# Scaling gate and up products in place in PSUM, with the low-rank matmul accumulated onto them

## What is computed

```
def _qlinear(x, q, scale, A, Bm):
    w = (q.astype(jnp.float32) - Q_ZERO) * (scale * Q_STEP)[:, None]
    y = jnp.einsum('bsh,oh->bso', x, w)
    return y + LR_SCALE * (x @ A @ Bm)
g = _qlinear(x, gate_q, gate_scale, gate_A, gate_B)
u = _qlinear(x, up_q, up_scale, up_A, up_B)
h = jax.nn.silu(g) * u
return _qlinear(h, down_q, down_scale, down_A, down_B)
...
x = x + 0.5 * _L0_ffn_ref(_layernorm(x), ...)
x = x + _L0_attn_ref(_layernorm(x), ...)
x = x + 0.5 * _L0_ffn_ref(_layernorm(x), ...)
```

## Time and profile before

| | |
|---|---|
| median of 3 runs | 631.45 us (631.31 to 633.48) |
| span of the profiled execution | 632.9 us |
| busy PE, DVE, ACT, POOL | 601.7, 457.9, 270.9, 72.3 us |
| instructions on PE, DVE, ACT, POOL | 3070, 851, 505, 89 |
| mean granted TensorE clock | 0.992 of full speed |
| DMA | 35.46 MB |

### The profile page before, as it was taken

One profiled execution on the slowest core, in us unless ns is written; L12 is line 12 of the kernel. 1 busy time (PEld: TensorE's weight loads), 2 busy tenths in 40 slices (PEclk: granted clock), 3 DMA queues, 4 the chain that ended last, 5 costly groups with the idle time before them and its releaser, 6 DMA issues.

```text
span 632.9 us, 9273 instructions
## 1 busy us (share of the span) xinstructions
PE 601.7 (95%) x3070; PEld 290.9 (46%) x3070; DVE 457.9 (72%) x851; ACT 270.9 (43%) x505; POOL 72.3 (11%) x89
## 2 busy tenths in 40 slices
PE   3798899999999999999997999999999999999997
PEld 2443444444444545444454544444454444544443
DVE  6699949895788868793698589548874688556643
ACT  3765303662066404561563366216640565126620
POOL 4236800000000001000064000000000000000000
PEclk9999989999999999999997999999999999999999
DMA  8984120004000210000278000300031001250001
GB/s 298 395 279 132 39 46 1 2 1 76 8 0 0 50 33 2 1 1 2 49 140 141 21 2 1 75 9 2 1 55 29 0 0 27 56 200 0 1 9 59
DMA packets 67620, 35.46 MB, mean 56 GB/s; under 512 B 56160, under 2 KB 60448, under 8 KB 67584
## 3 DMA queue, kind: packets, MB, share of 16 engines
q1 hardware_dynamic: 66768, 34.87, 21.0%
q10 hardware_dynamic: 816, 0.14, 0.1%
HBM read 17.43 MB, written 4.19 MB: 34 GB/s over the span
## 4 chain that ended last, share of the span: by engine, by line
PE 79%; DVE 8%; issue 1%; ACT 1%; DVEq 1%; ACTq 0%
PE bank L1047 41%; PE bank L1025 22%; PE bank L1004 5%; PE bank L1065 5%; PE bank L981 2%; PE bank L1144 2%; PE bank L1126 1%; PE bank L1013 1%; DVE z L627 1%; DVE work L708 1%; DVE zs L620 1%; DVE X L670 1%; DVE X L911 1%; DVE uq_raw L667 0%; DVE z L629 0%
## 5 line engine op out<-in xcount | busy, mean ns | idle before, releaser
L512 ACT ACTIVATE work<-bank,scales 128x512 f32<-128x512 f32 (+1 forms) x176 | 120.3, 684 | 173.8 <-PE bank L1047 173.3
L1047 PE MATMUL bank<-xT,gw 128*128 128x512 f16 (+1 forms) x696 | 164.4, 379 | 0.8 <-ACT work L512 0.8
L1047 PE MATMUL bank<-xT,uw 128*128 128x512 f16 (+1 forms) x696 | 164.4, 379 | 0.0
L1025 PE MATMUL bank<-dw,hT 128*128 128x512 f16 (+1 forms) x704 | 160.6, 381 | 0.0
L1047 PEld LDWEIGHTS bank<-xT,gw 128*128 128x128 f16 (+1 forms) x696 | 69.4, 100 | 81.2 <-ACT work L512 1.6
L1047 PEld LDWEIGHTS bank<-xT,uw 128*128 128x128 f16 (+1 forms) x696 | 69.7, 100 | 79.8
L1025 PEld LDWEIGHTS bank<-dw,hT 128*128 128x128 f16 (+1 forms) x704 | 68.1, 98 | 78.6 <-issue 2.2
L690 DVE SCALAR_TENSOR_TENSOR work<-bank,work 128x512 f32<-128x512 f32 (+1 forms) x88 | 60.6, 688 | 27.2 <-ACT work L512 21.3
L703 DVE SCALAR_TENSOR_TENSOR work<-bank,work 128x512 f32<-128x512 f32 (+1 forms) x88 | 60.4, 686 | 20.8 <-ACT work L512 20.4
L708 DVE TENSOR_TENSOR work<-work 128x512 f32<-128x512 f32 (+1 forms) x88 | 63.7, 724 | 4.7 <-ACT work L535 1.3
L648 DVE SCALAR_TENSOR_TENSOR hT<-work,hT 128x512 f16<-128x512 f32 (+1 forms) x88 | 61.2, 695 | 6.1 <-ACT hT L517 5.6
(11 more groups left out here) (145 smaller groups left out, 436.7 us busy)
## 6 DMA issues: line engine op xcount, KB each, us to landing
out_x<-X SPq DMA_DIRECT2D x16, 256.0 KB, 2.1
X<-in_x SPq DMA_DIRECT2D x1, 2048.0 KB, 14.8
gq_raw<-in_tables SPq DMA_DIRECT2D x1, 2048.0 KB, 11.7
gq_raw<-in_gate_q_t SPq DMA_DIRECT2D x2, 768.0 KB, 11.3
uq_raw<-in_up_q_t SPq DMA_DIRECT2D x2, 768.0 KB, 11.3
dq_raw<-in_down_q_t SPq DMA_DIRECT2D x1, 1536.0 KB, 14.6
work<-in_b SPq DMA_DIRECT2D x2, 688.0 KB, 8.4
X<-in_x SPq DMA_DIRECT2D x4, 256.0 KB, 5.3
```

The source lines that it names most:

```text
L512: return nc.scalar.activation(out, in_, ACT.Copy, scale=scales[0:rows[m], g, m:m + 1])
L1025: last = mm(bank[4 + b][:, :], hT[0:rows[m], m, a, j * P:(j + 1) * P], dw[0:rows[m], m, :], start=(m == 0 and a == 0), stop=(m == M - 1 an ...
L1047: last = mm(dst[0:r, :], w[:, c, cols], xT[:, a, c, :], start=(c == 0 and a == 0), stop=(c == KH - 1 and a == 1))
```

## The change

The gate product of block m goes to bank 0 or 2 and up's to bank 1 or 3, by m % 2. ACT multiplies each by its channel factor in place, PSUM to PSUM. The low-rank matmul of a block is issued one block later, without clearing, so that it adds to the scaled bank. Silu reads the gate bank, DVE multiplies its result with the up bank. L690 and L703 and four SBUF tiles are gone. The common factor `LR_OUT` moves into silu's scale, `h_high`, `h_low` and the channel factors. `pd_product` uses bank 2. At the end of a tile `down_half(n, 0, 0)` stands between the two halves of `pd_product`.

```diff
@@ scalar
-            def scaled(out, in_, g, m):
-                return nc.scalar.activation(out, in_, ACT.Copy, scale=scales[0:rows[m], g, m:m + 1])
+            def scaled(acc, g, m):
+                return nc.scalar.activation(acc, acc, ACT.Copy, scale=scales[0:rows[m], g, m:m + 1])
...
+            def gate_silu(n, m):
+                b, r = m % 2, rows[m]
+                act.wait_ge(f.gl_mm, n * M + m + 1)
+                after(act, f.h[b], uses(n, m))
+                nc.scalar.activation(silu[0:r, b, :], gate_bank[b][0:r, :], ACT.Silu, scale=LR_OUT)\
+                    .then_inc(f.silu[b], 1)
...
                 for m in range(M):
-                    b, r, k = m % 2, rows[m], uses(n, m)
+                    b, r = m % 2, rows[m]
                     act.wait_ge(f.g_mm, n * M + m + 1)
-                    after(act, f.g[b], k)
-                    scaled(tg[0:r, b, :], bank[0][0:r, :], 0, m).then_inc(f.tg[b], 1)
+                    scaled(gate_bank[b][0:r, :], 0, m).then_inc(f.tg[b], 1)
+                    if m:
+                        gate_silu(n, m - 1)
+                    act.wait_ge(f.u_mm, n * M + m + 1)
+                    scaled(up_bank[b][0:r, :], 1, m).then_inc(f.tu[b], 1)
                     if m:
                         h_high(n, m - 1)
...
+                gate_silu(n, M - 1)
                 h_high(n, M - 1)
@@ vector
-                    dve.wait_ge(f.tg[b], k + 1)
-                    dve.wait_ge(f.gl_mm, n * M + m + 1)
-                    after(dve, f.silu[b], k)
-                    V.scalar_tensor_tensor(g32[0:r, b, :], bank[2][0:r, :], c, tg[0:r, b, :],
-                                           ALU.mult, ALU.add).then_inc(f.g[b], 1)
+                    dve.wait_ge(f.ul_mm, n * M + m + 1)
+                    dve.wait_ge(f.silu[b], k + 1)
+                    after(dve, f.hlo[b], k)
+                    V.tensor_tensor(h32[0:r, b, :], silu[0:r, b, :], up_bank[b][0:r, :], ALU.mult)\
+                        .then_inc(f.h[b], 1)
                     if m:
                         h_low(n, m - 1)
...
@@ tensor
             def pd_product(n, half):
 
                 if half == 0:
-                    pe.wait_ge(f.tg[(M - 1) % 2], uses(n, M - 1) + 1)
+                    pe.wait_ge(f.silu[M % 2], uses(n, M - 2) + 1)
                     pe.wait_ge(f.hlo[0], uses(n, M - 3) + 1)
                     pe.wait_ge(f.hlo[1], uses(n, M - 4) + 1)
...
+                def product(g, m):
+                    b, r, cols = m % 2, rows[m], slice(m * P, m * P + rows[m])
+                    w, dst, done = ((gw, gate_bank[b], f.g_mm), (uw, up_bank[b], f.u_mm))[g]
+                    after(pe, (f.silu, f.h)[g][b], uses(n, m))
...
+                def low_rank(g, m):
+                    b, r, cols = m % 2, rows[m], slice(m * P, m * P + rows[m])
+                    w, dst, done = ((gb_w, gate_bank[b], f.gl_mm), (ub_w, up_bank[b], f.ul_mm))[g]
+                    pe.wait_ge((f.tg, f.tu)[g][b], uses(n, m) + 1)
...
+                    mm(dst[0:r, :], w[:, cols], PT[:, g, :], start=False, stop=True,
+                       skip_group_check=True).then_inc(done, 1)
+
+                started = first and n == 0
                 for m in range(M):
...
+                    for g in range(2):
+                        if not (started and m == 0):
+                            product(g, m)
+                        if m:
+                            low_rank(g, m - 1)
                     if s4 and m == 2:
                         cauchy(n)
...
                 pd_product(n, 0)
+                for g in range(2):
+                    low_rank(g, M - 1)
+                down_half(n, 0, 0)
                 pd_product(n, 1)
                 if more:
                     p_product(n + 1, 0)
-                down_half(n, 0, 0)
                 if more:
                     p_product(n + 1, 1)
                 down_half(n, 0, 1)
@@ sync
             def transposes(n):
 
-                sp.wait_ge(f.ul_mm, n * M)
+                sp.wait_ge(f.u_mm, n * M)
```

More of the change, by code:

```diff
@@ L243, in s4_macaron @@
         c_out = [sem(f"conv_out_{j}") for j in range(TS)]
+        gate_bank, up_bank = (bank[0], bank[2]), (bank[1], bank[3])
         c_bank = [bank[4], bank[5], bank[2], bank[3]]
@@ L500, in pd_high @@
                 after(act, f.dl_mm, n * TS)
-                nc.scalar.activation(PdT[:, :], bank[0][:, :], ACT.Copy,
+                nc.scalar.activation(PdT[:, :], bank[2][:, :], ACT.Copy,
                                      scale=1.0 / (H_SCALE * A_SCALE)).then_inc(f.pd_hi, 1)
@@ L699, in tile @@
                         down_a()
[L700 to L709, removed]
                     if more and m in (1, 3, 6, 8):
@@ L1003, in pd_product @@
                     for a in range(2):
-                        last = mm(bank[0][:, :], da_w[0:rows[m], m, :, :].rearrange("p a r -> p (a r)"),
+                        last = mm(bank[2][:, :], da_w[0:rows[m], m, :, :].rearrange("p a r -> p (a r)"),
                                   hT[0:rows[m], m, a, :], start=(m == 0 and a == 0),
@@ L1031, in tile @@
             def tile(n, more, s4=False, first=False):
-                for m in range(M):
[L1035 to L1069, removed]
-                        product(0)
-                    if not late:
-                        low_rank(0)
-                    if not started:
-                        product(1)
-                    if late:
-                        low_rank(0)
-                    low_rank(1)
@@ new lines, in product @@
+                def product(g, m):
+                    b, r, cols = m % 2, rows[m], slice(m * P, m * P + rows[m])
+                    w, dst, done = ((gw, gate_bank[b], f.g_mm), (uw, up_bank[b], f.u_mm))[g]
+                    after(pe, (f.silu, f.h)[g][b], uses(n, m))
+                    if m == 0 and g == 1:
+                        pe.wait_ge(f.p_stack, n * TS + TS)
+                    if first and m == 1 and g == 0 and n != 0:
+                        for out_read in c_out:
+                            pe.wait_ge(out_read, SUBS // TS)
+                    if isinstance(n, int) and n == 0:
+                        pe.wait_ge((s_gcast, s_ucast)[g], 1 + sum(m >= m1 for _, m1 in CHUNKS))
+                    for c in range(KH):
+                        for a in range(2):
+                            last = mm(dst[0:r, :], w[:, c, cols], xT[:, a, c, :],
+                                      start=(c == 0 and a == 0), stop=(c == KH - 1 and a == 1))
+                    last.then_inc(done, 1)
@@ new lines, in low_rank @@
+                def low_rank(g, m):
+                    b, r, cols = m % 2, rows[m], slice(m * P, m * P + rows[m])
+                    w, dst, done = ((gb_w, gate_bank[b], f.gl_mm), (ub_w, up_bank[b], f.ul_mm))[g]
+                    pe.wait_ge((f.tg, f.tu)[g][b], uses(n, m) + 1)
+                    if m == 0 and g == 0:
+                        if isinstance(n, int) and n == 0:
+                            pe.wait_ge(f.PT0, TS)
+                        else:
+                            for b_pt in range(2):
+                                pe.wait_ge(f.PT[b_pt], n * 32)
+                    if isinstance(n, int) and n == 0 and m == 0:
+                        pe.wait_ge(s_bw, g + 1)
+                    mm(dst[0:r, :], w[:, cols], PT[:, g, :], start=False, stop=True,
+                       skip_group_check=True).then_inc(done, 1)
@@ L1159, in first_products @@
                             last = mm(bank[g][:, cols], w[:, c, 0:P], xT[:, a, c, cols],
-                                      start=(c == 0 and a == 0), stop=(c == KH - 1 and a == 1))
+                                      start=(j == 0 and c == 0 and a == 0), stop=(c == KH - 1 and a == 1),
+                                      skip_group_check=True)
                     if j == TS - 1:
```

21 lines of the change are left out of this document (8 added, 13 removed).

## The result

| | before | after |
|---|---|---|
| median | 632.28 us (4 runs) | 657.46 us (4 runs, 656.4 to 658.43) |
| span of the profiled execution | 632.9 us | 656.7 us |

"Before" and "after" name the two kernels and their traces from here on. The ratio is 1.0389, with a 95% interval from 1.0362 to 1.0415: slower by 25.2 us. 657.3 was forecast. An execution's time is about 1.7 us over its span, as 658.43 to 656.7 in the profiled one of after. By the same 1.7 the profiled execution of before took some 634.6 us, more than its median (an estimate), so the two spans differ by less than the two medians.

What follows compares the result with a forecast made beforehand. TensorE was taken as the bound, busy 601.7 of 632.9 us, so only its idle counts. Stalls of 17.9 + 3.4 + 4.5 + 0 = 25.8 us gave a span of 658.7, less 1.45: 657.3 us, range 650 to 672.

Steps and rivals of the forecast that it cites:

- Steady tiles: Tiles 1, 2, 4, 5, 6: two new PE stalls each, 17.9 us more in all.
- The first stall: Tile end, ahead of pd_product's first half: PE waits for h_low(8), queued behind h(9) on DVE; 1.7 us a tile.
- the second: Ahead of the second p_product: PE waits for DVE's split with down_half's cover gone; 1.8 us a tile.
- T: Time at a tile's end when the next matmul follows the last product group; now low-rank (up, 9) is issued then.
- Tiles 3 and 7: These two tiles have only the stall ahead of pd_product: 3.4 us more together.
- cauchy: Tile 3 after block 2: PE waits 2.8 us for DVE's resolvents, plus 1.7 us of lower clock; 4.5 us more.
- Tile 0: The lighter DVE can remove 4.4 us of stalls, but the win waits at the second p_product; 0 taken.
- In-place scaling: Gate/up loop: scaling PSUM to PSUM takes about 0.69 us and costs nothing, under a cover 0.6 us wide.
- rival 2: The clock also falls at 12 short gaps ahead of pd_product and p_product in steady tiles: 668 us, chance 0.27.
- The rival in which the time moves on into other waits: The experiments' main rival: the three waits are one DVE chain, so mending one moves the time into the next.
- rival 5: DVE reaches h_low(8) early, so no first stall, a smaller second, and tile 0's 4.4 us won: 627 us, chance 0.04.

Runs made afterwards that it cites:

- e3_cauchy: The changed kernel with cauchy issued after block 3 of tile 3 instead of after block 2: 652.62 us.
- e2_cover: The changed kernel with down_half(n,0,1) moved between p_product(n+1,0) and p_product(n+1,1): 646.63 us.
- e9_order: The changed kernel with all three waits mended, silu's table loaded early, and ln_apply for token group 3 behind pd_split and the first p_split: 624.61 us.
- the first two experiments: The changed kernel with pd_product waiting only for low parts it reads, 646.65 us; separately, with down_half(n,0,1) between the two p_product, 646.63 us.
- the last two kernels: Changed kernel, three waits mended, plus early table load and later ln_apply of group 3: 624.61 us; kernel before with only those last two edits: 629.08 us.
- e6_before_nocover: The kernel before with down_half(n,0,0) issued ahead of p_product(n+1,0), so the two p_product stand back to back: 637.48 us.
- e1_wait: The changed kernel with pd_product waiting only for the low parts of h it reads, no more for h_low(8) at its start: 646.65 us.
- the two copies: The changed kernel with two more ScalarE copies (128 x 512) behind every scaling of gate: 686.07 us in a single run.

## Why the prediction was right, point by point

- **Steady tiles** (17.9 us forecast): 17.4. The first stall was 1.74 us for 1.7, the second 1.80 for 1.8. In the first, two small errors cancel: DVE starts h(9) 0.57 us after T and not 0.42, and PE starts 0.10 us behind `h_low(8)` and not 0.2. Both causes were tested alone and together.
- **Tiles 3 and 7** (3.4): about 3.2.
- **`cauchy`** (4.5): the wait was 2.58 us, and the 8 matmuls behind it took 1.65 us longer. From the start of tile 3 to `pd_product`'s first matmul is 45.14 us before and 50.17 after; less 1.6 for the wait there, and with 0.43 for two low-rank matmuls that have moved behind it, `cauchy` costs 3.9, as the 3.96 of e3_cauchy say. The forecast is 0.6 too high.
- **Tile 0** (0): 0.5 us more. As forecast, the end of the products comes earlier, and the second `p_product` at 80.70 for 80.23. One term was missed: the gap of 2.06 us ahead of the gate product of m=2 was foreseen, but not that the clock would fall behind it, 3.53 us for 1.89. It does not fall in every execution (below), so a part of this term's closeness is luck. The forecast also read PE's waits for DVE in this loop as 3.2 us in 4; L703 has one more, of 0.7 us. The 4.4 us that it used come from the starts of the matmuls and hold them all.
- **The convolution stage** (not in the sum): from the end of PE's longest wait there to tile 4 it takes 11.17 us instead of 12.26, fewer matmuls being slow behind a gap of the same length. It hides 1.1 us of the loss, and was not foreseen. Nothing here was tried on it. Behind the same wait the clock does not fall at all in the traces of e2_cover and e9_order (3.16 and 3.18 us), so this term differs between executions too.
- **In-place scaling** (nothing, cover 0.6 us): nothing; the cover is 0.7 to 0.8 us. The rule of the Trainium skill ("ScalarE: Activation LUTs", step-by-step section) that ScalarE reaches PSUM faster agrees in sign with 0.661 against 0.684 us.
- **The clock at short gaps** (rival 2): none of the 12 gaps of 1.43 to 1.78 us in tiles 1 to 7 lowered it; the granted clock of tile 1, with two of them, is 1.00. The swings that the Trainium skill ("TensorE: Matmul & The Clock Gate", psum-queue depth-cycling) describes did not show in steady tiles. The rival in which the time moves on into other waits fell with the first two experiments.
- **Faster** (rival 5): it needed `h_low(8)` before T. The order on DVE spoke against it, and the trace has it at 144.28. The gain that it named in tile 0 exists, as the last two kernels show, but only with the waits mended.

**Longer waits do not cost the same clock in every execution.** The forecast took 1.7 us from the one wait of 2.36 us in the trace of before. e6_before_nocover has the same wait at the same place, and no fall; e1_wait has after's gap of 2.06 us ahead of m=2, and no fall either:

```profile
80.47 0.61 PE L981 MATMUL bank<-a_w,xT 128*128 128x128 f16 x8 [2.36 <-DVE p_stack L635]
80.92 2.32 PE L1025 MATMUL bank<-dw,hT 128*128 128x512 f16 x10
```

```profile
29.77 1.90 PE L1046 MATMUL bank<-xT,gw 128*128 128x512 f16 x8 [2.06 <-ACT work L529]
```

The code of tile 0 is the same in after and in e3_cauchy, and from its first gate product to that of tile 1 it takes 88.14 and 86.41 us. So one trace cannot price such a gap to better than about 1.7 us. At `cauchy` the price held: behind waits of 2.57 to 2.72 us there the clock fell in all five traces that have one.

The sum was 25.8 us, the spans differ by 23.8 and the medians by 25.2. `cauchy` was 0.6 too high and the 1.1 us of the convolution stage were not in the sum; the steady tiles, 0.5 too high, tiles 3 and 7, 0.2 too high, and tile 0, 0.5 too low, make up the rest. The mechanism is shown; that the median comes within 0.2 us of 657.3 is in part luck, as the median of before was 631.45 us when the forecast was made and is 632.28 with one more run.

## What to carry to other kernels

When a result is formed one block later to save instructions, follow every wait at the end of the loop and at every side job within it: a semaphore that asks for more than the next instructions read, or a filler that has moved, costs its full latency in an engine that was never idle. Relieving an engine that nobody waits for gives nothing; here 120 us less of DVE work were worth some 4 to 6 us, nearly all of it in the one stage in which PE waited for DVE. Where a gap may lower the clock, look at the same gap in several traces before giving it a price. Before trusting a cover, write down its width, and if in doubt measure it by adding work, as with the two copies.

## What the runs showed of the hardware

- ScalarE from PSUM to the same place in PSUM, 128 x 512 float32 with a per-partition factor: 0.661 us, against 0.684 from PSUM into SBUF. Silu from PSUM with an immediate factor: 0.589.
- The clock of PE behind waits, in the 12 traces of this study after their first 20 us: behind 64 waits of 1.43 to 1.79 us it never fell. Behind 14 waits of 1.97 to 2.72 us it fell to the lower of its two levels 11 times, and behind 19 of 3.02 to 4.41 us 14 times. Where it fell, 8 matmuls took up to 3.54 us instead of 1.90 and 12 took 4.44 instead of 2.75; after 2.58 us the stretch of the slow matmuls has a mean clock of 0.53. The same wait can do either: 2.06 us at one place gave 3.53 us for 8 matmuls in after and 1.90 in e1_wait, and 2.36 us gave 3.62 us for 10 in before and 2.32 in e6_before_nocover. The fall may come late: behind after's gap of 3.39 us the first 8 small matmuls still took 0.61 us, and the 10 behind them 4.01 instead of 2.32.
- One more ScalarE copy of 128 x 512 in each block, 0.5 us, was free in all steady tiles; a second one cost 0.32 us a block.
